# A four-layer graph network on one Trainium2 core: attention over targets from broadcast 16-bit keys, and a last layer that gathers by tiles of 128 edges

## The reference, cut to what matters

```python
# layer 0, attention over the edges of each target node, 4 heads of 16 columns
g = leaky_relu(xl[src] + xr[dst] + edge_attr_16 @ W_e, 0.2)
logits = einsum('ehc,hc->eh', g, att)
amax = segment_max(logits, dst)
ex = exp(logits - amax[dst])
alpha = ex / (segment_sum(ex, dst)[dst] + 1e-16)
out = segment_sum(xl[src] * alpha[..., None], dst)
# layer 3: messages go from the column node dst to the row node src
m = relu(h[dst] + edge_attr_64)
agg = segment_sum(m, src)
```

## Time and profile before

| | us |
|---|---|
| median of 3 runs | 26595.03 |
| lowest and highest | 26588.95, 26601.55 |
| the profiled execution | 26592.22 |
| its span in the profile | 26590.5 |

### The profile page before, as it was taken

One profiled execution on the slowest core, in us unless ns is written; L12 is line 12 of the kernel. 1 busy time (PEld: TensorE's weight loads), 2 busy tenths in 40 slices (PEclk: granted clock), 3 DMA queues, 4 the chain that ended last, 5 costly groups with the idle time before them and its releaser, 6 DMA issues. The chain is left out here.

```text
span 26590.5 us, 540850 instructions
## 1 busy us (share of the span) xinstructions
PE 19464.4 (73%) x107861; PEld 12610.8 (47%) x107889; DVE 16052.1 (60%) x58888; ACT 7043.9 (26%) x24344; POOL 16506.8 (62%) x17229
## 2 busy tenths in 40 slices
PE   5688888888888599999999677777777653333334
PEld 2344444444444355555556355555555433333332
DVE  7788888888888544444445566666666553333333
ACT  0233333333333122222222133333333211111111
POOL 0377777777777377777776255555555437777772
PEclk9555555555555555555555588888888755555555
DMA  7122222222225233333334466666666712222233
GB/s 289 28 44 43 43 44 43 44 43 43 44 43 43 40 76 76 76 76 76 76 76 64 52 110 110 108 109 108 109 111 109 89 30 60 60 60 60 60 56 21
DMA packets 2877529, 1894.36 MB, mean 71 GB/s; under 512 B 2008316, under 2 KB 2481378, under 8 KB 2869682
## 3 DMA queue, kind: packets, MB, share of 16 engines
q0 software_dynamic: 607024, 854.80, 19.9%
q1 hardware_dynamic: 2269906, 1034.48, 18.9%
HBM read 1573.79 MB, written 342.46 MB: 72 GB/s over the span
## 5 line engine op out<-in xcount | busy, mean ns | idle before, releaser
L1262 POOL DMA_INDIRECT H<-tab,a_rs x3520 | 3369.6, 957 | 2970.8 <-issue 2257.1
L850 POOL DMA_INDIRECT H<-tab,idx x3520 | 3387.3, 962 | 2050.0 <-issue 1062.5
L1621 POOL DMA_INDIRECT H<-tab,m_idx x3520 | 3346.6, 951 | 1668.4 <-issue 1022.1
L1793 POOL DMA_INDIRECT g_G<-tab,g_rs x3520 | 3331.7, 946 | 1619.4 <-issue 1059.2
L1545 POOL DMA_INDIRECT rec<-PT,posi x3125 | 3059.1, 979 | 1281.2 <-issue 1026.0
L1855 PE MATMUL g_ps_a<-g_zr,g_oh 128*128 128x64 f32 x7040 | 1712.6, 425 | 2872.7 <-issue 2048.6
L1855 PEld LDWEIGHTS g_ps_a<-g_zr,g_oh 128*128 128x128 f32 x7040 | 1567.5, 328 | 3018.2 <-issue 2240.5
L928 DVE CUSTOM_DVE_ANT_0 junk<-ps_lb,pen 128x512 bf16<-128x512 f32 x3520 | 2292.0, 689 | 845.2 <-PE ps_lb L1035 799.4
L1721 PEld LDWEIGHTS m_ps_a<-m_Sx,H 128*128 128x128 f32 x7040 | 1567.4, 328 | 1414.7 <-issue 1414.0
L1367 PE MATMUL a_ps_z<-a_w_ea,a_eaT 64*128 64x288 f32 x3520 | 1202.6, 466 | 1404.5 <-DVE a_z L1285 1388.3
L1067 PEld LDWEIGHTS ps_a<-V,H 128*128 128x128 f32 x7040 | 1567.2, 328 | 767.3 <-issue 767.3
(11 more groups left out here) (331 smaller groups left out, 40145.5 us busy)
## 6 DMA issues: line engine op xcount, KB each, us to landing
a_rs<-rec SPq DMA_DIRECT2D x880, 164.0 KB, 5.8
g_rs<-rec SPq DMA_DIRECT2D x880, 164.0 KB
rec<-H SPq DMA_DIRECT2D x46, 3116.0 KB
m_row<-key SPq DMA_DIRECT2D x880, 128.0 KB
H<-startp SPq DMA_DIRECT2D x880, 128.0 KB
a_row<-keyc SPq DMA_DIRECT2D x880, 128.0 KB
PT<-in_ea SPq DMA_DIRECT2D x625, 160.0 KB
H<-tab,idx POOLq DMA_INDIRECT x3520
```

Source lines behind the costliest of these rows:

```text
L850: pool.indirect_dma_start(G[:, k, t, :], None, table, bass.IndirectOffsetOnAxis(ap=idx[:, k, t, :], axis=0)).then_inc(s_g[k], 16)
L1262: pool.indirect_dma_start(G[:, k % SLOTS, t, 0:R], None, tab2, bass.IndirectOffsetOnAxis(ap=rs[:, k, t, 1:2], axis=0)).then_inc(s_g[k % SL ...
L1621: pool.indirect_dma_start(G[:, k, t, :], None, tab1, bass.IndirectOffsetOnAxis(ap=idx[:, k, t, :], axis=0)).then_inc(s_g[k], 16)
L1793: pool.indirect_dma_start(G[:, k, t, :], None, tab3, bass.IndirectOffsetOnAxis(ap=rs[:, k, t, 1:2], axis=0)).then_inc(s_g[k], 16)
```

## The change

- **Setup** makes a second table, for tiles of 128 edges instead of groups of 512: for each of NT = 3232 tiles its block of nodes and its first record. VectorE and TensorE do this in 7 slices of up to 512 tiles, right after `goff` and ahead of the places. Each slice is put in one of two buffers (`ti`) and stored to a new tensor `tiles` in DRAM by two DMAs of SyncE's queue. Of the 3232 tiles, 3170 hold edges (counted from the inputs).
- **Layer 0** is a function of its own, `target_attention`. SyncE also loads the group's keys as 16-bit numbers, broadcast to all partitions (`row`). VectorE compares these with the partition's number, which gives the turned one-hot `ohN` directly, and makes the straight one in float32 itself. TensorE's four transposes of the one-hot and two of ScalarE's three copies are gone, and the penalty is made from `ohN`. The scores that are spread and the running maximum are single bf16 numbers: the low parts are gone, the matmuls of line 1059 are 4 instead of 8, and the exponent is clamped at 70 instead of 1.
- **Layer 3** goes over the tiles, four at a time in 808 rounds. SyncE reads each tile's first record with a register load of its own and loads the tile with a DMA of its own. TensorE keeps the four sums of a round apart, and VectorE adds each to its block's accumulator, with a register load for each.

```diff
+    NT = (E + NBLK * (P - 1)) // P
+    NT = -(-NT // (SLOTS * T)) * (SLOTS * T)
...
+        tiles = dram("tiles", (2, NT), I32)
...
                     for r in range(0, NG * T, RUN):
                         m = min(RUN, NG * T - r)
                         sp.dma_start(places[:, r:r + m, :], rinit[:, 0:m, :]).then_inc(s_rec, 16)
+                    for c in range(NTS):
+                        a, b = 512 * c, min(NT, 512 * c + 512)
+                        sp.wait_ge(s_ti, c + 1)
+                        for o in range(2):
+                            sp.dma_start(tiles[o:o + 1, a:b], ti[0:1, c % 2, o, 0:b - a]).then_inc(s_tst[c % 2], 16)
                     sp.wait_ge(s_rec, 16 * n_rec)
...
+                    for c in range(NTS):
+                        a, b = 512 * c, min(NT, 512 * c + 512)
+                        q, m = c % 2, b - a
+                        at_least(dve, s_tsum, c - 1)
+                        dve.tensor_scalar(past[:, q, 0:m], giota[:, 0:m], float(a), tcol[:, 0:1], ALU.add, ALU.is_ge).then_inc(s_tp, 1)
+                        dve.wait_ge(s_tsum, c + 1)
+                        at_least(dve, s_tst[q], 32 * (c // 2))
+                        do(dve.tensor_scalar(ti[:, q, 0, 0:m], ps_t[:, 0, 0:m], float(NB), None, ALU.min))
+                        at_least(dve, s_ti, c)
+                        do(dve.scalar_tensor_tensor(fo[:, 0:m], giota[:, 0:m], float(a), ps_t[:, 1, 0:m], ALU.add, ALU.add))
+                        do(dve.tensor_scalar(fo[:, 0:m], fo[:, 0:m], float(P), float((NG * T - 1) * P), ALU.mult, ALU.min))
+                        dve.tensor_copy(ti[:, q, 1, 0:m], fo[:, 0:m]).then_inc(s_ti, 1)
...
-                        def onehot(g, k, r):
-                            q = k % 2
+                        def onehots(g, k, r):
+                            at_least(dve, s_me, g - SLOTS + 1)
+                            at_least(dve, s_pen, g - SLOTS + 1)
+                            settle(dve)
+                            dve.tensor_scalar(ohN[:, k], row[:, k], base_node[:, 0, bass.ds(g, 1)], pcol[:], ALU.subtract, ALU.is_equal).then_inc(s_ohN, 1)
                             dve.wait_ge(s_lo, g + 1)
-                            at_least(dve, s_ohT, g - 1)
-                            at_least(dve, s_oh32, g - 1)
+                            at_least(dve, s_acc, g - SLOTS + 1)
                             for t in range(T):
-                                ins = dve.tensor_scalar(ohb[:, q, t, :], iota_b[:], lo[:, t:t + 1], None, ALU.is_equal)
+                                ins = dve.tensor_scalar(oh[:, k, t, :], iota_b[:], lo[:, t:t + 1], None, ALU.is_equal)
                             ins.then_inc(s_oh, 1)
...
                         def edge_maxima(g, k, r):
-                            pe.wait_ge(s_mh, g + 1)
-                            pe.wait_ge(s_ml, g + 1)
+                            pe.wait_ge(s_mn, g + 1)
...
                         def node_sums(g, k, r):
-                            pe.wait_ge(s_oh32, g + 1)
+                            pe.wait_ge(s_oh, g + 1)
                             pe.wait_ge(s_V, g + 1)
...
-                            sp.dma_start(rs[:, k], rec[bass.ds(g * GE, GE), :].rearrange("(p t) c -> p t c", p=P)).then_inc(s_ld[k], 16)
-                        steps(sp, NG, body)
+                            for t in range(T):
+                                e = sp.value_load(tab[0:1, 1, bass.ds(g * T + t, 1)], min_val=0, max_val=(NG * T - 1) * P)
+                                sp.dma_start(rs[:, k, t, :], rec[bass.ds(e, P), :]).then_inc(s_ld[k], 16)
+                        steps(sp, NGT, body)
...
+                            for t in range(T):
+                                blk_t = dve.value_load(tab[0:1, 0, bass.ds(g * T + t, 1)], min_val=0, max_val=NB)
+                                acc = ACC[:, bass.ds(blk_t, 1), 0:D].rearrange("p a c -> p (a c)")
+                                if t == 0:
+                                    dve.wait_ge(s_acc, g + 1)
+                                at_least(dve, s_done, g * T + t)
+                                dve.tensor_tensor(acc, acc, ps_a[:, k % 2, t, 0:D], ALU.add).then_inc(s_done, 1)
```

More of the change, by code:

```diff
@@ L344, in program @@
             s_eap = sem_in(ctx, "features_copied")
+            tcol = sb_in(ctx, "tcol", [P, 2])
+            ti = sb_in(ctx, "ti", [P, 2, 2, 512], I32)
+            ps_t = ps_all[:, 1536:2560].rearrange("p (k c) -> p k c", k=2)
+            NTS = -(-NT // 512)
+            s_tp, s_tsum, s_ti = (sem_in(ctx, n) for n in ("tile_blocks_past", "tile_sums", "tile_rows"))
+            s_tst = [sem_in(ctx, f"tile_rows_stored{q}") for q in range(2)]
             NSL = -(-NG // 512)
@@ L570, in _ @@
                     pe.wait_ge(s_tab, 3 * NSL)
+                    for c in range(NTS):
+                        m = min(NT, 512 * c + 512) - 512 * c
+                        pe.wait_ge(s_tp, c + 1)
+                        at_least(pe, s_ti, c)
+                        pe.matmul(ps_t[:, 0, 0:m], ones[:], past[:, c % 2, 0:m], start=True, stop=True)
+                        pe.matmul(ps_t[:, 1, 0:m], tcol[:, 1:2].broadcast_to([P, P]), past[:, c % 2, 0:m], start=True, stop=True).then_inc(s_tsum, 1)
                     pe.wait_ge(s_dig, NR)
@@ L723, in _, with target_attention @@
                         steps(act, NB, body, 2)
-        def attention(layer, order, table, heads, width, we, n_val):
+        def target_attention():
+            table, heads, width, n_val, order = tab0, HEADS, D, D, 0
             R = table.shape[1]
-            PT = PT2 if layer == 2 else PT1
+            PT = PT1
             VC = n_val // heads + 1
-            v0 = R - n_val
-            banks = 1 if T * width <= 512 else 2
-            tpb = T // banks
-            att = rows[:, ROWS["att"]] if layer == 0 else rows[:, ROWS["w_att2"]]
+            att = rows[:, ROWS["att"]]
@@ L757, in attention @@
[L757 to L762 removed]
+                key = sbl("key", [P, SLOTS, T], I32)
+                idx = sbl("idx", [P, SLOTS, T, 1], I32)
+                ea = sbl("ea", [P, SLOTS, T, DE])
+                row = sbl("row", [P, SLOTS, GE], I16)
@@ L802, in attention @@
-                s_lb = [seml(f"scores_spread{h}_") for h in range(heads)]
-                if layer == 0:
-                    filler = scatter_fill(ctx, 2, 0, (1, 3), (2, 0), (1, 0), ROUNDS)
-                else:
-                    filler = None
-                s_gm = [seml(f"group_max{h}_") for h in range(heads)]
+                ps_ea = ps_in(ctx, "t_ps_ea", [P, 512])
+                ps_lT = ps_in(ctx, "t_ps_lT", [P, 2 * GE], BF16)
+                ps_z = ps_in(ctx, "t_ps_z", [P, T, width])
@@ L809, in attention, with tile_of @@
+                s_lb = [seml(f"scores_spread{h}") for h in range(heads)]
+                s_gm = [seml(f"group_max{h}") for h in range(heads)]
+                filler = scatter_fill(ctx, 2, 0, (1, 3), (2, 0), (1, 0), ROUNDS)
+                def tile_of(a, t):
+                    return a.rearrange("n (p t) -> n t p", t=T)[:, t, :]
                 with nc.Block() as block:
@@ L830, in _ @@
-                        if filler:
-                            steps(sp, NG, body, fill=lambda k, r: filler.load(sp, k, r), filled=filler.rounds)
-                        else:
-                            steps(sp, NG, body)
+                            e = sp.value_load(goff[0:1, bass.ds(g, 1)], min_val=0, max_val=E)
+                            sp.dma_start(idx[:, k, :, 0], srcp[bass.ds(e, GE)].rearrange("(p t) -> p t", p=P)).then_inc(s_ld[k], 16)
+                            sp.dma_start(row[:, k, :], key16[bass.ds(e, GE)].partition_broadcast(P)).then_inc(s_ld[k], 16)
@@ L1147, in body @@
                             stage(features, -2, NG, *at)
-                            stage(copies, -2, NG, *at)
-                        features(0, 0, 0)
-                        copies(0, 0, 0)
-                        features(1, 1, 0)
-                        copies(1, 1, 0)
-                        if layer == 0:
-                            kept(0, 0, 0)
-                        if filler:
-                            filler.first(act)
-                            pipeline(act, NG, body, 2, fill=lambda k, r: filler.keys(act, k, r), filled=filler.rounds)
-                        else:
-                            pipeline(act, NG, body, 2)
+                            stage(penalty, 0, NG, *at)
+                        for g in range(2):
+                            features(g, g, 0)
+                        kept(0, 0, 0)
+                        filler.first(act)
+                        pipeline(act, NG, body, 2, fill=lambda k, r: filler.keys(act, k, r), filled=filler.rounds)
         def source_attention():
@@ L1776, in _ @@
                     def _(sp):
+                        for o in range(2):
+                            sp.dma_start(tab[0:1, o, :], tiles[o:o + 1, :]).then_inc(s_tab, 16)
+                        sp.wait_ge(s_tab, 32)
```

308 lines of the change are left out of this document (116 added, 192 removed).

## The result

The changed kernel takes **25648.68 us** (median of 4 runs, 25625.29 to 25658.01) against 26591.99 us for the kernel before in the same session: ratio 0.9644, 95% interval 0.963 to 0.9658. The forecast was 26620 us, 26380 at the least. The profiled execution has a span of 25654.3 us.

A forecast was written before the change was run, and what follows sets the result against it. It took no engine as busy throughout and read three stages: the setup's wait, layer 0's hand-over loop and layer 3's gathers on GpSimd. 26592.2 + 249 + 114 - 335 = 26620 us, range 26380 to 26870.

The forecast's parts named there:

- No measurable change: Whole kernel: the time stays within about 0.2% (53 us) of the kernel before; chance 0.22.
- every sign of being wrong that I named: Layer 0: GpSimd never waits at a period of 8.3 us; setup: VectorE passes the table without a long wait.
- Setup, +249: Setup: VectorE's third table slice waits for a store behind the records until 506 us; digits at 528 us instead of 279.
- The mild form: Setup: the small store lands at 441 us, ahead of the last records, making the term 184 us; total 26555 us.
- Rival B: Setup: the records hold nobody up, so it costs only its 35 us; total 26406 us; chance 0.10.
- Layer 0, +114: Layer 0: a new loop through VectorE and TensorE sets 8.78 us a group, +0.13 for each of 880 groups.
- the chain's 8.52: Layer 0: pieces from maximum through weighting, node sums, one-hot, reductions and spread back to maximum sum to 8.52 us.
- the terms of 0.05, 0.06 and 0.03: Layer 0, us a turn: one more semaphore 0.05, mean above the followed turn 0.06, the rest further waits of three engines.
- in every fourth turn VectorE reads two registers: Layer 0: a wait of about 0.5 us, hidden before, shows in every fourth turn: +0.12 us on the mean.
- Rival A: Layer 0 falls to GpSimd's pace, 8.30 us a group: -310 us instead of +114, total 26196 us; chance 0.15.
- Layer 3, -335: Layer 3: fewer tiles, 792.5 rounds with edges at 5.12 us and 15.5 without at 6.56: 4159 us against 4500.
- Rival C: Layer 3: SyncE's register loads and DMAs bind, 5.4 us a round or more: +222 us, total 26842; chance 0.15.

The follow-up runs named there:

- e17: Kernel before with 48 memsets on VectorE ahead of layer 2's loop, on a chip like the first: 25607.28 us, ratio 0.9631.
- e1: Changed kernel with 200 memsets more on VectorE ahead of layer 2's loop, on a slow chip: ratio 1.0151 to the kernel before.
- e4: Changed kernel with the tile table stored by ScalarE's queue instead of SyncE's, on a slow chip: ratio 0.9972 to the kernel before.
- e10: Changed kernel with tile table stored by ScalarE's queue, layer 0's one-hot compared late and layer 3's loads on two queues: 25321.36 us, ratio 0.9523.
- e8: Changed kernel with layer 0's float32 one-hot compared behind the maxima, exponents and weighting instead of ahead of the maxima: 25558.91 us.
- e9: Changed kernel with layer 3's four record loads a round split between ScalarE's and SyncE's queues: 25619.67 us.
- e13: Changed kernel with table stored by ScalarE's queue, late one-hot, block numbers read under the reductions, layer 3's loads on two queues; slow chip: ratio 0.9444.
- e3: Kernel before with 256 memsets on VectorE ahead of layer 2's loop, on a slow chip: ratio 1.0008 to the kernel before.
- e2: Kernel before with 90 memsets on VectorE ahead of layer 2's loop, on a slow chip: ratio 0.9931 to the kernel before.
- e7: Changed kernel again, unaltered, on a chip like the first: 25654.60 us, ratio 0.9647 to the kernel before.
- e12: Changed kernel with layer 0's block numbers read under the reductions and the one-hot compared late, on a slow chip: ratio 0.9611 to the kernel before.
- e11: Changed kernel with layer 0's block numbers read behind the second and fourth reductions, on a slow chip: ratio 0.9865 to the kernel before.

## Why the prediction was wrong

- **What bounds the kernel.** I read three stages, since the diff touches three. Layer 2 was costed at nothing without reading its rows, and not even named: that is the step that failed. In its place the runs showed that VectorE's loop there had been fetched anew each time round, and that the change moved it by 48 instructions to a place where it isn't: 992 us with nothing else changed (e17). Its -1003 us is more than the whole error of 971. The sum without it, 26592 + 64 = 26656, is 36 us from the forecast; that is this close in part by luck, since layer 0 is 83 us above its term and layer 3 49 us below. In the trace of the kernel before, two rows showed it: 578 instruction packets, and VectorE's 321 us of "issue" in 2000 us of layer 2.
- **No rival covered it.** "No measurable change" and every rival took the untouched layers as fixed, and every sign of being wrong that I named lay in the three touched stages. A change of the length of a program ahead of a long loop is a way of its own in which a time can go, in either direction: e1 shows the loss, e17 the gain.
- **Setup, +249:** right, 251, with the idle time (210 us) and the digits (530.7) where forecast. The mild form, by which the small store would land at 441 us, did not come: it was issued at 445.7 and landed at 506. e4 shows that SyncE's queue is the cause. Rival B was wrong as to this kernel, and right in what it is worth to get rid of the wait: 214 us by its sum, 200 in e10.
- **Layer 0, +114:** the mechanism was right, the size was not: +197. The three turns without a second load were forecast at 8.66 on the mean (the chain's 8.52 and the terms of 0.05, 0.06 and 0.03) and took 8.69. Mis-sized is the term "in every fourth turn VectorE reads two registers": I gave it 0.5 us in such a turn, 0.12 on the mean; it is 0.77 (9.46 against 8.69), 0.19 on the mean. Of the 0.10 us between 8.78 and 8.88 that is 0.07, and the other 0.03 lie in the chain. Rival A took 8.3 for what is left without the loop; e8 shows that cutting the loop alone gives 0.11 us a turn on the mean: its turns with one load fall to 8.3 to 8.6 us, but the loads stand in the way of the fourth.
- **Layer 3, -335:** right, -384; a round took 5.06 us, not 5.12. Rival C fell on this chip (e9: SyncE costs 0.06 us a round) and holds in part on the slow ones (e13: the split takes 482 us off layer 3).
- Against the kernel before with its code well placed (e17) the change costs some 40 us, where I had forecast 28: of what it touches, "gains and losses cancel" was right.

## What to carry to other kernels

Read the row of the instruction queue before anything else: if its packets are many, some loop may be fetched anew in every turn, and an "issue" of 4 to 10 us once a turn on the engine with the long body was its mark here. Then the length of *any* code ahead of it can change the time, and two kernels can only be compared stage by stage. Shift the loop, or shorten its body (here 8 groups unrolled; no run tried that), and judge a change with the placement held equal. Beside that: a store that frees a buffer must not stand behind bulk DMAs in the program of one queue. And register loads belong behind an operation long enough to hide them, not in a chain that goes round; how much that brings is only estimated here, on a slow chip.

## What the runs showed of the hardware

- **Loading of code.** A loop of 327 instructions on VectorE was fetched anew in every turn at four placements (0, 90, 256, and 248 instructions from where it lay before) and stayed in at two (48, 176). Packets are 8192 bytes (4.73 MB in 578), and 48 and 176 differ by 128. The loop goes back 107 times, and each time 5 packets came in, at all four bad placements. The wait was 8.9 us each time in the kernel before and 7.0 in e3, with two packets starting within it, and 4.1 to 4.2 in e1 and e2, with one. In all it cost 992 us (e17 against the kernel before). The Trainium skill (Runtime: NRT & Kernel Launch, Instruction fetch mechanics) says that instructions come in 16 KiB blocks of 256 into a small memory, 32 KiB for most engines, and that a taken branch out of the two blocks present forces a fetch. The runs agree that the branch of a loop can force it. They don't agree with 256 as the unit. With blocks of 256, the starts from which a loop overruns two blocks form one stretch on a circle of 256, whatever its length. Shifts of 0 and 90 reload, so one of the two ways between them would have to reload throughout; but 48 lies on the one way and 176 on the other, and both do well. That the unit is 128, with 3 units that fit and 4 that don't, is inferred from these six placements, and 176 is the only new placement that it forecast; no run measured either number by itself.
- **The granted clock** of layer 2 was 0.87 with the stalls and 0.96 to 0.97 without, TensorE's program being the same. It is a mean of its two levels, 1.2 and 2.4 GHz; how long it ran at the upper one was decided by VectorE's stalls, in which TensorE idles.
- **Chips.** The same kernel before took 26590 us on some chips and 34900 to 35900 on others. There SyncE's rows show instructions that stretch (the DMA of line 850 took 0.70 us beside 0.33 for the next; in e7 the same one never took over 0.37). And VectorE has waits of 4 to 6 us that the profile can put down to no instruction ("remote"), where its longest wait of the same stretch in e7 is 0.9 us:

```profile
7011.81 0.70 SPq L850 DMA_DIRECT2D t_idx<-srcp  x1
7012.56 0.33 SPq L851 DMA_DIRECT2D t_row<-key  x1
```

```profile
DVE t_dd L940 <- remote: 197.8, 38, 5.9
DVE H L889 <- remote: 158.8, 38, 4.3
```

(Both of e4: timeline of SyncE's queue, and waits from 7000 to 8000 us.) Of layer 0's turns every second one is hit: in e1 four turns take 17.6, 8.6, 18.4 and 8.7 us. Why is open. It matters for the change: the late one-hot was worth 954 us there (e12 against e11) and 96 on a chip like the first; that this is because each slow wait hits the whole chain is not shown. And the gain of the change itself is one of chips like the first. On the chip of e1 to e4 layer 3 got longer, 5838 and 5923 us (e4, e1) against 5409 and 5426 (e3, e2), and e4's ratio is 0.9972; with e1's later start of 206 us the changed kernel would come out at about 1.004 there, as an estimate.
